# Laying out a stack of queries and its maxima by DMA through DRAM scratch instead of by selection products

## The chip, the cores and the metric

The kernel runs on one core of one Trainium2 chip. The metric is device time in microseconds of one launch. In the profile PE is TensorE (matrix products), PEld its weight loads, DVE VectorE, ACT ScalarE, POOL GpSimd, and SP is SyncE, which here issues every DMA.

## The reference

Sixteen sequences of 256 tokens with 128 channels go through four layers, each with a layer norm ahead and a residual behind: a linear attention with decay ("a"), a feed-forward layer ("ffn"), a causal softmax attention ("b"), and the same feed-forward layer again. The change lies in attention b:

```python
q = (x @ Wq + bq).reshape(Bx, Tx, HEADS, HD)      # 16 heads of 8
k = (x @ Wk + bk)[:, :, None, :]                  # one key head for all
v = (x @ Wv + bv)[:, :, None, :]
q, k = _apply_rope(q, sin, cos, HD), _apply_rope(k, sin, cos, HD)
att = jnp.einsum('bthd,bThd->bhtT', q, k) / math.sqrt(HD)
att = jax.nn.softmax(jnp.where(causal, -jnp.inf, att), axis=-1)
out = jnp.einsum('bhtT,bThd->bthd', att, v).reshape(Bx, Tx, Cx)
return out @ Wo + bo
# ffn: acc = sum over 8 experts of (silu(x @ wg) * (x @ wu)) @ wd, hidden size 512
```

## The kernel before

The 4096 tokens are cut into NT = 8 tiles of TOK = 512 tokens (two sequences, SPT = 2). The feed-forward layers set the pace: each tile passes through 8 experts x 4 chunks of 128 hidden columns = 32 units (UNIT), and the whole program is one list of slots, one unit per slot. Units 0 to 255 are the first feed-forward layer, then come 4 slots without a unit (GAP), then units 256 to 511. In each slot TensorE does the three gate products of its unit (point 0 follows), the three up products (point 1), and the three down products of the unit three slots back (point 2, LAG = 3). Every operand is split in a high part, rounded to float32r, and a low part, the rest, so each product is three.

The two attentions are fitted in between. A table gives every step of a tile a slot r, counted from the tile's own slot 0 (for b that is b_slot(t)), a point in the slot and a bank of PSUM (A_CELL L134, B_CELL L138). Slots -22 to 35 of one b tile overlap with those of the next, 32 slots later. Each engine walks the slots in order and, within a slot, runs its parts in the order in which its loop names them; waits on semaphores do the rest. Nothing is reordered by a planner.

A b tile, in slots r: layer norm and its turn (-22 to -19); q, k and their rope partners projected (-8 to -6); VectorE multiplies by the cosine and sine tables (`rope_b`), GpSimd adds the two (QK, -6 and -5, L624), ScalarE rounds to the high half (QKH, -5 and -4, L807), VectorE subtracts for the low half (QKL, -4 and -3, L1414). The heads have 8 channels, so a product over one head would use 8 of 128 rows. Instead the kernel stacks, for each of four groups g of 32 partitions (RG), the parts high, high, low of one head's query (8 rows each, 24 in all) and two rows for a maximum; the keys stand beside it as high, low, high and two rows of ones. One product over 32 rows then gives the exact sum and, in the second pass, subtracts the row's maximum. Four heads j lie side by side in the columns.

These stacks are made by selection products: `query_stack` (L1097, cells qst0 to qst3, slots -3 and -2) and `key_stack` (L1102, cell kst, slot -1) multiply by matrices of ones and zeros in SELR, and ScalarE copies the result to QST (L812) and KST (L816). `rows` (slots 0 to 11) then computes the masked scores by rows, VectorE takes their negated maxima (L1362) and splits them into a zeroed tile NMP (`split_maxima`). `stack2` (L1070, four cells per tile, slots 7, 9, 14, 15) adds to a copy of QST the turned maxima, by products with an identity, and ScalarE copies that to Q2 (L828). `cols` (slots 12 to 23) computes the scores again by columns, with the maximum subtracted; ScalarE takes the exponential (`exps`), GpSimd cuts what lies above the diagonal (`cut_weights` L595), and `values` (slots 18, 19, 24, 25) multiplies by v.

GpSimd's loop over the slots (L689 to L697) runs, in each slot, the low half HL of the unit one slot back (`hidden_lo` L536), then its part of attention a, then that of b with the cuts. SyncE reloads the weights of one expert (1.5 MB, L512) as soon as the down products have freed one of three buffers, in a plain loop over the loads, and stores a finished tile now and then. The loads fall in the slots r = -6, -2, 2, 6, ... of a b tile.

Of the kernel before, what the change touches and what calls it, by code (L numbers as in the profile page):

```python
# [14 lines left out]
P = 128  # L15
# [13 lines left out]
RG = 32  # L29
# [7 lines left out]
def constants():  # L37
# [24 lines left out]
    r = np.arange(P)  # L62
    c["mask_rows"] = np.where(r[None, :] > r[:, None], MASKED, 0.0)
    c["mask_cols"] = np.where(r[:, None] > r[None, :], MASKED, 0.0)

    for j in range(NJ):
        hi = np.zeros((P, P), np.float32)
        lo = np.zeros((P, P), np.float32)
        for g in range(NG):
            for x in range(DB):  # L70
                src = (NJ * g + j) * DB + x
                hi[src, RG * g + x] = hi[src, RG * g + DB + x] = lo[src, RG * g + 2 * DB + x] = 1
        c[f"qhi_{j}"], c[f"qlo_{j}"] = hi, lo
    hi = np.zeros((P, P), np.float32)
    lo = np.zeros((P, P), np.float32)
    for g in range(NG):
        for x in range(DB):
            hi[x, RG * g + x] = hi[x, RG * g + 2 * DB + x] = lo[x, RG * g + DB + x] = 1
    c["khi"], c["klo"] = hi, lo
    ones = np.zeros((P, P), np.float32)  # L80
    for g in range(NG):
        ones[0, RG * g + 3 * DB:RG * g + 3 * DB + 2] = 1
    c["kone"] = ones
    c["eye"] = eye
# [11 lines left out]
C_SEL = CPOS["qhi_0"][0]  # L96
SELS = [f"q{p}_{j}" for j in range(NJ) for p in ("hi", "lo")] + ["khi", "klo", "kone", "eye"]
# [30 lines left out]
def unit_of(g):  # L128
# [10 lines left out]
          "qst0": (-3, 1, 0), "qst1": (-3, 2, 1), "qst2": (-2, 1, 2), "qst3": (-2, 2, 0), "kst": (-1, 1, 1),  # L139
          ("stack", 0, 0): (7, 1, 3), ("stack", 0, 1): (9, 1, 3), ("stack", 1, 0): (14, 1, 3),  # L140
          ("stack", 1, 1): (15, 1, 3), ("pv", 0, 0): (18, 1, 3), ("pv", 0, 1): (19, 0, 3), ("sums", 0, 0): (20, 1, 3),
# [70 lines left out]
def program(nc, a_x, a_Wq, a_Wk, a_Wv, a_Wbeta, a_bbeta, a_Wmix, a_bmix, a_Wout, a_bout, a_ln_g, a_ln_b,  # L212
            b_Wq, b_bq, b_Wk, b_bk, b_Wv, b_bv, b_Wo, b_bo, f_Wg, f_Wu, f_Wd, consts, out):
    ctx = ExitStack()
    with ctx:
# [31 lines left out]
        ONESR = sb("ONESR", [1, TOK], F32R)  # L247
# [9 lines left out]
        SELR = sb("SELR", [P, 2 * NJ + 4, P], F32R)  # L257
# [27 lines left out]
        kept_sel = nc.dram_tensor("kept_sel", [P, len(SELS) * P], F32)  # L285
# [10 lines left out]
        def here(name, offset, *shape, dt=F32):  # L296
# [38 lines left out]
        NMP = take("NMP", 2, 2, NJ, P, dt=F32R)  # L335
# [6 lines left out]
        Q2 = take("Q2", 2, NJ, SEQ, dt=F32R)  # L342
# [12 lines left out]
        ld = sems("ld", "x0 x1 x tables masks sel0 sel wa wb ba bb raw0 raw1")  # L355
# [7 lines left out]
        B = sems("b", "proj roped u_q u_k hi lo v_ready v_used st_ready st_used kst_ready kst_used row_ready row_used nmh nml "  # L363
                      "q2_ready q2_used t_ready t_used t_cut pv os turn ro o ot otc out biased done")
# [62 lines left out]
        def consumed(key):  # L427
# [15 lines left out]
            if name in ("qst0", "qst1", "qst2", "qst3"):  # L443
                return B.st_used, NJ * t + int(name[3]) + 1
            if name == "kst":
                return B.kst_used, t + 1
            if name == "v":
# [4 lines left out]
                    "stack": lambda: (B.q2_used, 2 * n + name[2] + 1),  # L452
# [20 lines left out]
        def _(sp):  # L473
# [15 lines left out]
            sp.dma_start(kept_sel[:, :], consts[:, C_SEL:]).then_inc(ld.sel0, 16)  # L489
# [8 lines left out]
            sp.wait_ge(ld.sel0, 16)  # L498
            sp.dma_start(SELR[:, :, :].rearrange("p a b -> p (a b)").bitcast(F32), kept_sel[:, :]).then_inc(ld.sel, 16)
            sp.dma_start(MRAW[:, :, :].rearrange("p a b -> p (a b)"), consts[:, C_MASK:C_SEL]).then_inc(ld.masks, 16)  # L500
# [5 lines left out]
            for x in range(NE, 2 * NT * NE):  # L506
# [6 lines left out]
                if x % NE == 4 and x // NE > NT:  # L513
                    t = x // NE - NT - 1
                    sp.wait_ge(F.done, NT + t + 1)
                    sp.dma_start(o_tok[:, t], X[:, t, :, :]).then_inc(stored, 16)
# [5 lines left out]
        def _(g):  # L522
# [85 lines left out]
            def side_b(t, r):  # L608
# [16 lines left out]
                for b in range(SPT):  # L625
                    for i, (at, point) in enumerate(COLS_AT[b]):
                        if r == at + (point == 2) + 1:
                            cut_weights(SPT * t + b, i)
# [3 lines left out]
            def early(slot):  # L632
# [33 lines left out]
                if slot == first + 7:  # L666
                    g.tensor_copy(ONESR[:, 0:P], ONES[0:1, :]).then_inc(pr.mask, 1)
                    for k in range(1, SUB):
                        g.tensor_copy(ONESR[:, k * P:(k + 1) * P], ONES[0:1, :]).then_inc(pr.mask, 1)
# [9 lines left out]
                if slot == a_slot(NT - 1) + 10:  # L679
                    g.wait_ge(A.proj, len(PROJ) * NT)  # L680
                    g.memset(NMP[:, :, :, :, :].rearrange("p a b c d -> p (a b c d)").bitcast(F32),
                             0.0).then_inc(pr.zero, 1)
                    g.memset(VF[:, :, :], 0.0).then_inc(pr.zero, 1)
# [5 lines left out]
            for slot in range(G_FIRST, G_LAST + 1):  # L689
                n = unit_of(slot - 1)  # L690
                if n is not None and on_pool(n):
                    hidden_lo(n)
                for t, r in a_tiles(slot):
                    side_a(t, r)
                for t, r in b_tiles(slot):
                    side_b(t, r)
                early(slot)  # L697

        @block.scalar
        def _(act):  # L700
# [94 lines left out]
            def side_b(t, r):  # L795
# [7 lines left out]
                if r in (-5, -4):  # L803
                    i = r + 5
                    act.wait_ge((B.u_q, B.u_k)[i], t + 1)
                    after(act, B.kst_ready, t)
                    act.activation(QKH[:, i, :], QK[:, i, :], ACT.Copy).then_inc(B.hi, 1)  # L807
                for j, at in enumerate((-3, -2, -2, -1)):
                    if r == at:
                        act.wait_ge(B.st_ready, NJ * t + j + 1)  # L810
                        after(act, B.q2_ready, 4 * t)
                        act.activation(QST[:, j, :], sbank[bank_of(("b", t, f"qst{j}"))], ACT.Copy).then_inc(B.st_used, 1)  # L812
                if r == -1:
                    act.wait_ge(B.kst_ready, t + 1)
                    after(act, B.t_ready, 8 * t)
                    act.activation(KST[:, :], sbank[bank_of(("b", t, "kst"))], ACT.Copy).then_inc(B.kst_used, 1)  # L816
                for b in range(SPT):
# [6 lines left out]
                    for h in range(2):  # L824
                        if r == B_CELL["stack", b, h][0]:
                            act.wait_ge(B.q2_ready, 2 * n + h + 1)
                            after(act, B.t_ready, 4 * (n - 1))
                            act.activation(Q2[:, b, 2 * h:2 * h + 2, :], r3(sbank[bank_of(("b", t, ("stack", b, h)))], 2),  # L828
                                           ACT.Copy).then_inc(B.q2_used, 1)
# [18 lines left out]
            for slot in range(G_FIRST, G_LAST + 1):  # L848
# [22 lines left out]
                if slot == a_slot(NT - 1) + 11:  # L871
                    act.wait_ge(pr.zero, 2)
# [6 lines left out]
        def _(pe):  # L879
            SQ, SL, SK, SKL, SKONE, SID = 0, 1, 2 * NJ, 2 * NJ + 1, 2 * NJ + 2, 2 * NJ + 3  # L880
# [124 lines left out]
            def rows(t, b, i):  # L1005

                if (b, i) == (0, 0):
                    pe.wait_ge(B.kst_used, t + 1)
                    pe.wait_ge(B.st_used, NJ * (t + 1))
                q = [QST[g * RG:(g + 1) * RG, :, b * SEQ:(b + 1) * SEQ] for g in range(NG)]  # L1010
                ks = [KST[g * RG:(g + 1) * RG, b * SEQ:(b + 1) * SEQ] for g in range(NG)]
# [11 lines left out]
            def cols(t, b, i):  # L1023

                n = SPT * t + b
                if i == 0:
                    pe.wait_ge(B.q2_used, 2 * (n + 1))
                for x, (part, g) in enumerate(THREES[i]):
                    rg = slice(g * RG, (g + 1) * RG)
                    key = KST[rg, b * SEQ + P:(b + 1) * SEQ] if part == 0 else KST[rg, b * SEQ:b * SEQ + P]  # L1030
                    q2 = Q2[rg, b, :, P:SEQ] if part == 0 else Q2[rg, b, 2 * (part - 1):2 * part, :]
# [38 lines left out]
            def stack2(n, b, h, bk):  # L1070

                pe.wait_ge(B.nml, 2 * (n + 1))
                for x in range(2):
                    j = 2 * h + x
                    dst = bk[:, x * SEQ:(x + 1) * SEQ]
                    pe.matmul(dst, SELR[:, SID, :], QST[:, j, b * SEQ:(b + 1) * SEQ], start=True, stop=False)  # L1076
                    for a in range(2):
                        m = pe.matmul(dst[:, a * P:(a + 1) * P], NMP[:, b, a, j, :], SELR[:, SID, :],  # L1078
                                      start=False, stop=(a == 1))
                m.then_inc(B.q2_ready, 1)  # L1080
# [16 lines left out]
            def query_stack(t, j, bk):  # L1097
                pe.wait_ge(B.lo, 2 * t + 1)
                pe.matmul(bk, SELR[:, SQ + 2 * j, :], QKH[:, 0, :], start=True, stop=False)
                pe.matmul(bk, SELR[:, SL + 2 * j, :], QKL[:, 0, :], start=False, stop=True).then_inc(B.st_ready, 1)  # L1100

            def key_stack(t, bk):  # L1102
                pe.wait_ge(B.lo, 2 * (t + 1))
                pe.matmul(bk, SELR[:, SK, :], QKH[:, 1, :], start=True, stop=False)
                pe.matmul(bk, SELR[:, SKL, :], QKL[:, 1, :], start=False, stop=False)
# [441 lines left out]
```

## Time and profile before

| | |
|---|---|
| median of 3 runs | 1659.95 us (1657.62 to 1661.47) |
| the profiled execution, its own time | 1660.08 us |
| its span, first to last instruction | 1658.4 us |
| TensorE's mean granted clock | 0.976 of full |
| PE, DVE, ACT, POOL busy | 1506.3, 1174.4, 886.4, 792.4 us |
| GpSimd's HL, waiting for ScalarE's HH | 550.2 us in 266 waits |
| DMA engines, mean busy share | 36% |

Busy time of TensorE is modelled: a product of 512 columns is shown with some 0.39 us, but the starts of two in a row lie 0.23 us apart, since they are pipelined. So times of products are read from start to start. A wait in the tables is named by the instruction that waited and by the one that ended the wait.

### The profile page before, as it was taken

What the parts mean: (1) busy time and instruction counts of PE and PEld (TensorE: products, weight loads), DVE (VectorE), ACT (ScalarE), POOL (GpSimd) and SP (SyncE); (2) the same over time, 40 slices, a digit from 0 to 9 for tenths busy, and PEclk for the clock granted to TensorE, in tenths of its full rate; (3) what the DMA queues carried; (4) which work ended last, traced back from release to release, by engine and by line L of the source; (5) the groups of instructions that cost most, each with busy time, mean ns of one, the idle gap of its engine ahead of it and who ended that gap; (6) DMA issues with size and microseconds to landing.
All of it is one profiled execution on the core that took longest, in us unless ns stands there. A gap on an engine that the chain in (4) does not pass through costs nothing. (4 is left out here: it accounts for less than half of the span.)

```text
span 1658.4 us, 23396 instructions
## 1 busy us (share of the span) xinstructions
PE 1506.3 (91%) x7528; PEld 1115.0 (67%) x7528; DVE 1174.4 (71%) x1943; ACT 886.4 (53%) x1520; POOL 792.4 (48%) x742
## 2 busy tenths in 40 slices
PE   2478999899999998899999999999999999999998
PEld 2366777677777777676666776766767677676676
DVE  4778787868787787878685584765847658477565
ACT  2245556464655555455646555565555555655554
POOL 2636444643525253433226545455465554645565
PEclk9689999999999999999999999999999999999999
DMA  6305543433433343433323332333333323333353
GB/s 193 124 1 185 201 153 115 153 119 148 153 140 128 148 152 120 153 115 118 126 99 115 115 136 104 148 121 115 115 121 121 129 103 150 121 115 122 140 178 115
DMA packets 36238, 216.68 MB, mean 131 GB/s; under 512 B 3476, under 2 KB 17301, under 8 KB 19733
## 3 DMA queue, kind: packets, MB, share of 16 engines
q1 hardware_dynamic: 36116, 215.18, 35.6%
q8 instruction: 62, 1.02, 0.2%
q14 instruction: 60, 0.48, 0.1%
HBM read 200.49 MB, written 15.47 MB: 130 GB/s over the span
## 5 line engine op out<-in xcount | busy, mean ns | idle before, releaser
L539 POOL TENSOR_TENSOR HL<-HF,HH 128x512 fp32r<-128x512 f32 x312 | 415.6, 1332 | 554.8 <-ACT HH L719 550.2
L1233 DVE TENSOR_TENSOR HF<-SG,bank 128x512 f32<-128x512 f32 x512 | 350.0, 684 | 169.1 <-PE bank L886 87.6
L884 PE MATMUL bank<-XTH,W 128*128 128x512 f32 x1024 | 423.6, 414 | 10.4 <-ACT SG L712 9.9
L886 PE MATMUL bank<-XTH,W 128*128 128x512 f32 x1024 | 403.8, 394 | 0.0
L885 PE MATMUL bank<-XTL,W 128*128 128x512 f32 x1024 | 403.3, 394 | 0.0
L1216 DVE SCALAR_TENSOR_TENSOR SG<-SG,bank 128x512 f32<-128x512 f32 x288 | 197.1, 684 | 242.9 <-ACT SG L714 241.2
L714 ACT ACTIVATE SG<-bank 128x512 f32<-128x512 f32 x288 | 172.2, 598 | 322.1 <-PE bank L886 320.6
L719 ACT ACTIVATE HH<-HF 128x512 fp32r<-128x512 f32 x512 | 320.2, 625 | 35.1 <-DVE HF L1233 31.1
L712 ACT ACTIVATE SG<-bank 128x512 f32<-128x512 f32 x224 | 133.6, 596 | 247.6 <-PE bank L886 246.3
L884 PEld LDWEIGHTS bank<-XTH,W 128*128 128x128 f32 x1024 | 194.5, 190 | 82.6 <-issue 22.5
L884 PE MATMUL dbank<-HH,W 128*128 128x512 f32 x512 | 218.9, 427 | 14.6 <-DVE HL L1222 13.4
L886 PEld LDWEIGHTS bank<-XTH,W 128*128 128x128 f32 x1024 | 194.2, 190 | 43.6
L885 PEld LDWEIGHTS bank<-XTL,W 128*128 128x128 f32 x1024 | 194.9, 190 | 35.8
L886 PE MATMUL dbank<-HH,W 128*128 128x512 f32 x512 | 202.3, 395 | 0.0
L885 PE MATMUL dbank<-HL,W 128*128 128x512 f32 x512 | 202.0, 394 | 0.0
L1222 DVE TENSOR_TENSOR HL<-HF,HH 128x512 fp32r<-128x512 f32 x200 | 166.8, 834 | 0.0
L884 PEld LDWEIGHTS dbank<-HH,W 128*128 128x128 f32 x512 | 97.4, 190 | 54.8 <-DVE HL L1222 18.0
L1362 DVE TENSOR_REDUCE NM<-three 128x12 f32<-128x1536 f32 (+2 forms) x96 | 114.1, 1216 | 13.0 <-PE three L1019 7.5
L1269 DVE TENSOR_TENSOR_SCAN S<-BETA,KV 128x512 f32<-128x512 f32 x80 | 117.7, 1476 | 0.1
L886 PEld LDWEIGHTS dbank<-HH,W 128*128 128x128 f32 x512 | 97.1, 190 | 21.7
L576 POOL TENSOR_TENSOR S<-S,PQ 128x512 f32<-128x512 f32 x40 | 62.9, 1576 | 95.1 <-DVE S L1269 95.1
L885 PEld LDWEIGHTS dbank<-HL,W 128*128 128x128 f32 x512 | 97.7, 191 | 13.9
(219 smaller groups left out, 1813.3 us busy)
## 6 DMA issues: line engine op xcount, KB each, us to landing
W<-kept_w SPq DMA_DIRECT2D x120, 1536.0 KB, 6.3
kept_w<-W SPq DMA_DIRECT2D x8, 1536.0 KB, 6.2
X<-in_L_attn_a_x_dram SPq DMA_DIRECT2D x8, 256.0 KB, 5.9
WS<-in_L_ffn_Wg_dram SPq DMA_DIRECT2D x8, 256.0 KB, 6.5
WS<-in_L_ffn_Wu_dram SPq DMA_DIRECT2D x8, 256.0 KB, 6.8
WS<-in_L_ffn_Wd_dram SPq DMA_DIRECT2D x8, 256.0 KB, 7.1
out_dram<-X SPq DMA_DIRECT2D x8, 256.0 KB, 7.2
CST<-in_tables_dram SPq DMA_DIRECT2D x1, 896.5 KB, 4.9
```

The lines of the kernel that those rows point to most:

```text
L539: g.tensor_tensor(HL[:, n % HRING, :], HF[:, n % HFRING, :], HH[:, n % HRING, :].bitcast(F32), ALU.subtract).then_inc(F.hl, 1)
L712: act.activation(SG[:, n % 2, :], fbank[2 * n % 3], ACT.Silu).then_inc(F.sil, 1)
L714: act.activation(SG[:, n % 2, :], fbank[2 * n % 3], ACT.Tanh, scale=0.5).then_inc(F.sil, 1)
L719: act.activation(HH[:, n % HRING, :], HF[:, n % HFRING, :], ACT.Copy).then_inc(F.hh, 1)
L884: pe.matmul(dst, wh, xh, start=start, stop=False)
L885: pe.matmul(dst, wh, xl, start=False, stop=False)
L886: return pe.matmul(dst, wl, xh, start=False, stop=stop)
L1216: v.scalar_tensor_tensor(gated, gated, 1.0, fbank[2 * n % 3], ALU.add, ALU.mult).then_inc(F.half, 1)
L1222: v.tensor_tensor(HL[:, n % HRING, :], HF[:, n % HFRING, :], HH[:, n % HRING, :].bitcast(F32), ALU.subtract).then_inc(F.hlv, 1)
L1233: v.tensor_tensor(HF[:, n % HFRING, :], gated, fbank[(2 * n + 1) % 3], ALU.mult).then_inc(F.mul, 1)
L1269: v.tensor_tensor_scan(S[:, m, c, :], BETA[:, m, :], KV[:, c, :], 0.0, ALU.mult, ALU.add).then_inc(A.scan, 1)
L1362: v.tensor_reduce(dst, src, AX.X, ALU.max, negate=True).then_inc(B.row_used, 1)
```

## The change

The tables of selection matrices and their SBUF tile SELR, NMP, Q2 and the row of ones go. Two scratch tensors in DRAM come (kept_q, kept_m), and three columns in the tables. The queries' high and low halves are stored to kept_q by SyncE and fetched back, rearranged, into QST: eight transfers for the high half, four for the low. The keys, which the projection already repeats on all partitions, are made in place: VectorE forms QK or QK - QKH by a column of factors, and ScalarE scales and adds ones by two more columns. The maxima are split side by side (NMS), turned by one product per sequence, copied by ScalarE to MT, stored to kept_m and fetched into the two free rows of QST itself, in four transfers per sequence. `rows` and `cols` take 24 and 26 rows of a group. SyncE's loop goes by slots. In GpSimd's loop the cuts and its part of b stand ahead of HL.

```diff
 B_CELL = {... "v": (-5, 1, 1),
-          "qst0": (-3, 1, 0), "qst1": (-3, 2, 1), "qst2": (-2, 1, 2), "qst3": (-2, 2, 0), "kst": (-1, 1, 1),
-          ("stack", 0, 0): (7, 1, 3), ("stack", 0, 1): (9, 1, 3), ("stack", 1, 0): (14, 1, 3),
-          ("stack", 1, 1): (15, 1, 3), ("pv", 0, 0): ...
+          ("mx", 0): (7, 1, 3), ("mx", 1): (14, 1, 3), ("pv", 0, 0): ...
+        kept_q = nc.dram_tensor("kept_q", [2, P, TOK], F32)
+        kept_m = nc.dram_tensor("kept_m", [SPT, 32, SEQ], F32)
...
+            def spread_queries(t, part, src, done):
+                for g in range(NG):
+                    to = RG * g + DB * part
+                    rows = kept_q[src, RG * g:RG * (g + 1), :].rearrange("(j x) t -> x j t", j=NJ)
+                    sp.dma_start(QST[to:to + DB, :, :].bitcast(F32), rows).then_inc(done, 16)
+            def spread_maxima(n, b):
+                sp.wait_ge(B.mt_out, 32 * (n + 1))
+                rows = kept_m[b].rearrange("(r g j) t -> g r j t", r=2, g=NG)
+                for g in range(NG):
+                    to = RG * g + 3 * DB
+                    sp.dma_start(QST[to:to + 2, :, b * SEQ:(b + 1) * SEQ].bitcast(F32),
+                                 rows[g]).then_inc(B.mrow, 16)
+            def side_b(t, r):
+                if r == -5:
+                    sp.wait_ge(B.hi, 2 * t + 1)
+                    after(sp, B.st_hi, 8 * 16 * t)
+                    sp.dma_start(kept_q[0], QKH[:, 0, :].bitcast(F32)).then_inc(B.hi_out, 16)
+                if r == -4:
+                    sp.wait_ge(B.hi_out, 16 * (t + 1))
+                    after(sp, B.t_ready, 8 * t)
+                    spread_queries(t, 0, 0, B.st_hi)
+                    spread_queries(t, 1, 0, B.st_hi)
+                    sp.wait_ge(B.lo, 2 * t + 1)
+                    after(sp, B.st_lo, 4 * 16 * t)
+                    sp.dma_start(kept_q[1], QKL[:, 0, :].bitcast(F32)).then_inc(B.lo_out, 16)
+                if r == -3:
+                    sp.wait_ge(B.lo_out, 16 * (t + 1))
+                    spread_queries(t, 2, 1, B.st_lo)
+                for b in range(SPT):
+                    n = SPT * t + b
+                    if r == B_CELL["mx", b][0]:
+                        sp.wait_ge(B.mt, n + 1)
+                        after(sp, B.mrow, 4 * 16 * (n - 1))
+                        for a in range(2):
+                            sp.dma_start(kept_m[b, :, a * P:(a + 1) * P],
+                                         MT[32 * a:32 * (a + 1), b, :].bitcast(F32)).then_inc(B.mt_out, 16)
+                    if r == B_CELL["mx", b][0] + 1:
+                        spread_maxima(n, b)
+            for slot in range(0, G_LAST + 1):
+                for t, r in b_tiles(slot):
+                    side_b(t, r)
+                for x in range(NE, 2 * NT * NE):
+                    u = FC * (x - WRING + 1) - 1
+                    if slot == ffn_slot(u // UNIT) + u % UNIT + LAG:
+                        load_weights(x)
...
@@ gpsimd
             for slot in range(G_FIRST, G_LAST + 1):
+                for t, r in b_tiles(slot):
+                    ... cut_weights(SPT * t + b, i) where r == at + (point == 2) + 1
+                    side_b(t, r)
                 n = unit_of(slot - 1)
                 if n is not None and on_pool(n):
                     hidden_lo(n)
                 for t, r in a_tiles(slot):
                     side_a(t, r)
-                for t, r in b_tiles(slot):
-                    side_b(t, r)
@@ scalar
-                        act.activation(QST[:, j, :], sbank[bank_of(("b", t, f"qst{j}"))], ACT.Copy).then_inc(B.st_used, 1)
-                    act.activation(KST[:, :], sbank[bank_of(("b", t, "kst"))], ACT.Copy).then_inc(B.kst_used, 1)
+                if r == -2:
+                    act.wait_ge(B.lo, 2 * (t + 1))
+                    act.activation(KST[:, :], B1[:, 1, :], ACT.Identity, bias=cst("k_one"),
+                                   scale=cst("k_keep")).then_inc(B.kst_used, 1)
+                    if r == B_CELL["mx", b][0]:
+                        act.wait_ge(B.mx, n + 1)
+                        act.activation(MT[0:64, b, :], sbank[bank_of(("b", t, ("mx", b)))][0:64, 0:P],
+                                       ACT.Copy).then_inc(B.mt, 1)
@@ tensor, rows
                     pe.wait_ge(B.kst_used, t + 1)
-                    pe.wait_ge(B.st_used, NJ * (t + 1))
-                q = [QST[g * RG:(g + 1) * RG, :, b * SEQ:(b + 1) * SEQ] for g in range(NG)]
+                    pe.wait_ge(B.st_hi, 8 * 16 * (t + 1))
+                    pe.wait_ge(B.st_lo, 4 * 16 * (t + 1))
+                q = [QST[g * RG:g * RG + 3 * DB, :, b * SEQ:(b + 1) * SEQ] for g in range(NG)]
@@ tensor, cols
-                    pe.wait_ge(B.q2_used, 2 * (n + 1))
+                    pe.wait_ge(B.mrow, 4 * 16 * (n + 1))
-            def stack2(n, b, h, bk): ...
+            def turn_maxima(n, b, bk):
+                pe.wait_ge(B.nml, n + 1)
+                pe.transpose(bk[0:64, 0:P], NMS[:, b, :].bitcast(F32), ident).then_inc(B.mx, 1)
-            def query_stack(t, j, bk): ...
-            def key_stack(t, bk): ...
@@ vector, split_b
+                else:
+                    v.scalar_tensor_tensor(B1[:, 1, :], QKH[:, 1, :].bitcast(F32), cst("k_lo"),
+                                           QK[:, 1, :], ALU.mult, ALU.add).then_inc(B.lo, 1)
```

## Rows read from the trace of the kernel before

**Rows 1.** Page part 1: busy us (share of the span) and instructions

```profile
PE 1506.3 (91%) x7528; PEld 1115.0 (67%) x7528; DVE 1174.4 (71%) x1943; ACT 886.4 (53%) x1520; POOL 792.4 (48%) x742
```

**Rows 2.** One tile's stretch: PE, PEld, DVE, ACT, POOL busy; clock, DMA share, GB/s

```profile
966.00:1072.00 106.00, 102.19 (x566) 72.88 (x563) 69.12 (x121) 59.78 (x100) 56.78 (x54) 1.00 0.33 122
```

**Rows 3.** Waits of TensorE from 730 to 1560: us, times, longest

```profile
PE abank L1039 <- POOL PT L605: 21.7, 14, 1.7
PE three L1099 <- DVE QKL L1414: 2.6, 7, 0.7
...
PE three L1099 <- DVE XTL L1210: 1.7, 1, 1.7
```

**Rows 4.** Timeline of TensorE, slots -3 to 0: start, length, instruction [idle before]

```profile
936.88 0.47 PE L1099 MATMUL three<-QKH,SELR 128*128 128x512 f32 x1 [0.30 <-DVE QKL L1414]
...
938.56 0.40 PE L1099 MATMUL three<-QKH,SELR 128*128 128x512 f32 x1
...
939.03 0.39 PE L884 MATMUL bank<-XTH,W 128*128 128x512 f32 x1
...
943.41 0.39 PE L1104 MATMUL three<-QKH,SELR 128*128 128x512 f32 x1
...
944.39 0.50 PE L884 MATMUL dbank<-HH,W 128*128 128x512 f32 x1
...
947.24 0.82 PE L999 MATMUL three<-MASKB 128*128 128x512 bf16 x3
```

**Rows 5.** Timeline of TensorE, two groups of maxima products and what follows

```profile
967.46 0.28 PE L1076 MATMUL abank<-QST,SELR 128*128 128x256 f32 x1
...
968.09 0.45 PE L884 MATMUL dbank<-HH,W 128*128 128x512 f32 x1
...
974.01 0.38 PE L1076 MATMUL abank<-QST,SELR 128*128 128x256 f32 x1
...
974.74 0.44 PE L884 MATMUL dbank<-HH,W 128*128 128x512 f32 x1
```

**Rows 6.** Timeline of TensorE, four transposes and what follows

```profile
931.09 0.66 PE L1052 MATMUL abank<-CST,OS 128*128 128x128 f32 x4
931.50 0.48 PE L884 MATMUL dbank<-HH,W 128*128 128x512 f32 x1
```

**Rows 7.** Timeline of GpSimd ahead of a `values` cell

```profile
1000.22 1.28 POOL L539 TENSOR_TENSOR HL<-HF,HH 128x512 fp32r<-128x512 f32 x1 [1.05 <-ACT HH L719]
1001.46 0.86 POOL L605 TENSOR_SCALAR_AFFINE_SELECT PT<-PT 128x768 f32<-128x768 f32 x1
```

**Rows 8.** Timeline of ScalarE, the queries' high half

```profile
930.36 0.62 ACT L807 ACTIVATE QKH<-QK 128x512 fp32r<-128x512 f32 x1
```

**Rows 9.** Stretches during and behind a weight load, columns as in rows 2

```profile
930.50:933.50 3.00, 3.00 (x22) 2.75 (x22) 1.41 (x4) 0.48 (x1) 2.52 (x2) 1.00 0.96 397
934.50:942.50 8.00, 7.70 (x35) 6.02 (x35) 6.27 (x14) 4.83 (x10) 3.88 (x3) 1.00 0.00 0
```

**Rows 10.** Timeline of SyncE: two issues in a row, and the last store

```profile
6.48 0.43 SPq L482 DMA_DIRECT2D GB<-in_L_attn_a_ln_g_dram  x1
6.95 0.43 SPq L483 DMA_DIRECT2D GB<-in_L_attn_a_ln_b_dram  x1
...
1655.65 0.39 SPq L518 DMA_DIRECT2D out_dram<-X  x1
```

**Rows 11.** DMA issues: KB each, median us from issue to landing

```profile
WRAW<-in_L_attn_a_Wq_dram SPq DMA_DIRECT2D x1, 64.0 KB, 1.8
```

**Rows 12.** Stretches behind two idle times of TensorE, columns as in rows 2

```profile
732.00:734.00 2.00, 1.76 (x8) 1.45 (x9) 0.78 (x2) 0.60 (x1) 0.00 (x0) 1.00 0.00 0
...
184.00:189.30 5.30, 5.30 (x15) 4.20 (x14) 3.38 (x6) 2.76 (x6) 0.00 (x0) 0.50 0.25 104
```

**Rows 13.** Timeline of TensorE in that stretch: first and thirteenth of the products

```profile
184.09 0.78 PE L884 MATMUL dbank<-HH,W 128*128 128x512 f32 x1
...
189.36 0.41 PE L884 MATMUL bank<-XTH,W 128*128 128x512 f32 x1
```

More of the change, by code:

```diff
@@ L62, in constants @@
     r = np.arange(P)
+    part = r % RG // DB
+    c["k_lo"] = np.where(part == 1, -1.0, 0.0)[:, None]
+    c["k_keep"] = np.where(part < 3, 1.0, 0.0)[:, None]
+    c["k_one"] = np.where((r % RG == 3 * DB) | (r % RG == 3 * DB + 1), 1.0, 0.0)[:, None]
     c["mask_rows"] = np.where(r[None, :] > r[:, None], MASKED, 0.0)
     c["mask_cols"] = np.where(r[:, None] > r[None, :], MASKED, 0.0)
[L66 to L84, printed above, removed]
     return {k: np.asarray(v, np.float32) for k, v in c.items()}
@@ L334, in program @@
         at["now"] = arena
-        NMP = take("NMP", 2, 2, NJ, P, dt=F32R)
+        NMS = take("NMS", 2, 64, dt=F32R)
+        MT = take("MT", 2, P, dt=F32R)
         VF = take("VF", SUB, RG)
@@ L442, in consumed @@
                 return bproj_read(t, name)
[L443 to L446, printed above, removed]
             if name == "v":
@@ L451, in consumed @@
                     "cols": lambda: (B.t_used, 4 * n + name[2] + 1),
-                    "stack": lambda: (B.q2_used, 2 * n + name[2] + 1),
+                    "mx": lambda: (B.mt, n + 1),
                     "pv": lambda: (B.os, 2 * n + name[2] + 1),
@@ L505, in _, with load_weights @@
             sp.dma_start(BRAW[:, C:], row(b_bk)).then_inc(ld.wb, 16)
-            for x in range(NE, 2 * NT * NE):
+            def load_weights(x):
                 sp.wait_ge(F.down, FC * (x - WRING + 1))
@@ new lines, in _ @@
+            for slot in range(0, G_LAST + 1):
[5 more added lines that the diff above has]
+                        load_weights(x)
+                        if x % NE == 4 and x // NE > NT:
+                            t = x // NE - NT - 1
+                            sp.wait_ge(F.done, NT + t + 1)
+                            sp.dma_start(o_tok[:, t], X[:, t, :, :]).then_inc(stored, 16)
@@ L665, in early @@
                     g.tensor_copy(MASKB[:, 1, :], ident).then_inc(pr.mask, 1)
[L666 to L669, printed above, removed]
                 if slot == first + 8:
@@ L689, in _ @@
             for slot in range(G_FIRST, G_LAST + 1):
+                for t, r in b_tiles(slot):
+                    for b in range(SPT):
+                        for i, (at, point) in enumerate(COLS_AT[b]):
+                            if r == at + (point == 2) + 1:
+                                cut_weights(SPT * t + b, i)
+                    side_b(t, r)
                 n = unit_of(slot - 1)
@@ L823, in side_b @@
                             act.activation(OS[:, z, :], abank, ACT.Copy).then_inc(B.os, 1)
[L824 to L829, printed above, removed]
+                    if r == B_CELL["mx", b][0]:
+                        act.wait_ge(B.mx, n + 1)
+                        after(act, B.mt_out, 32 * (n - 1))
+                        act.activation(MT[0:64, b, :], sbank[bank_of(("b", t, ("mx", b)))][0:64, 0:P],
+                                       ACT.Copy).then_inc(B.mt, 1)
                     if r == B_CELL["ot", b][0]:
@@ L1345, in maxima @@
             def maxima(n, b, i):
-                after(v, B.nml, 2 * (n - 1))
+                after(v, B.nml, n - 1)
                 v.wait_ge(B.row_ready, 4 * n + i + 1)
@@ L1374, in split_maxima @@
                 v.wait_ge(B.row_used, 6 * (n + 1))
[L1375 to L1383 removed]
+                after(v, B.mx, n - 1)
+                dst = NMS[:, b, :].rearrange("p (a r h) -> p a r h", a=2, r=2)
+                v.tensor_copy(dst[:, :, 0, :], NM[:, b, :, :]).then_inc(B.nmh, 1)
+                v.wait_ge(B.nmh, n + 1)
+                v.tensor_tensor(dst[:, :, 1, :], NM[:, b, :, :], dst[:, :, 0, :].bitcast(F32),
+                                ALU.subtract).then_inc(B.nml, 1)
             def gather_sums(n, a, bank):
```

97 lines of the change are left out of this document (20 added, 77 removed).

## The prediction, made before the changed kernel was run

> **What bounds the kernel now.** I read the page's engine table first: TensorE is busy for 91% of the span [rows 1]. An average over stages says little, so I next cut the span into stretches of one attention tile each. In one such stretch, 32 slots of some 3.3 us, TensorE is busy for 102.2 of 106 us at the full clock, VectorE for 69, ScalarE for 60, GpSimd for 57 [rows 2]. There are eight such tiles, and all that the change touches lies in them. So a product that goes there is worth its whole time, and a new wait of TensorE costs its whole time. The waits of TensorE in this part (from 730 us on) are few: 21.7 us in 14 waits for GpSimd's cut of the weights, 2.6 us in 7 for VectorE's low half of the queries [rows 3]. The program takes 1660.1 us by its own time, 1.7 more than the span; the median of three runs is 1659.95, so the sum needs no correction. About 0.2% (3.3 us) is what a measurement of this kernel tells from no change.
>
> **The change, part by part.**
>
> *Query stack.* Eight products of 512 columns per tile go. Two of them, with the next instruction's start, take 938.56 to 939.03 = 0.47 us [rows 4]; four pairs are 1.88 us. With them goes the wait for VectorE in front of the first (2.6 us in all).
>
> *Key stack.* Three products go, 943.41 to 944.39 = 0.98 us [rows 4], and the product behind them starts about 0.1 us late after the one-row operand: 1.08 us. In their place ScalarE scales by a column, where it copied; VectorE's second subtraction has one operand more. Both engines are at two thirds of the stretch or less.
>
> *Maxima.* Four groups of products per tile go; two of them took 0.63 and 0.73 us [rows 5], so 4 x 0.68 = 2.72. Two transposes come: four in the trace take 931.09 to 931.50 = 0.41 us [rows 6], so 0.1 us each, 0.2 per tile.
>
> Sum on TensorE: (1.88 + 1.08 + 2.72) x 8 = 45.4, less 1.7 for the transposes, plus 2.6: 46.3 us. Eight evacuations of ScalarE per tile and two small VectorE operations per sequence go too; neither engine is the bound, so I count them at nothing. What is late next where the stacks stood is VectorE, the next busiest [rows 2]: a few tenths per tile, by my estimate, which I leave in the range.
>
> *GpSimd's order.* The cut for a slot now stands ahead of that slot's low half HL. In the trace the HL from 1000.22 runs, and behind it from 1001.46 the cut for which TensorE waits [rows 7]. Before that HL, GpSimd waited 1.05 us for ScalarE, so the cut can begin 2.3 us sooner, more than the longest of the waits (1.7 [rows 3]). I take all 21.7 us. What is moved back by it is HL, by one cut (0.86 us [rows 7]) or, at r = -1, by the four small operations of a layer norm. HL is used two slots later, so this costs nothing; if that cover failed it would show as TensorE waiting for HL.
>
> All gains: 46.3 + 21.7 = 68.0 us, 8.5 per tile, which by themselves would give 1592.
>
> *The new path.* The queries now go out to DRAM and come back in twelve transfers, each into 8 partitions (four rows of 2 KB in each, 64 KB). Every step is on SyncE's queue and must land before the rows products of slot 0. In the tile that I followed they began at 947.24 [rows 4]; with 1.88 + 1.08 + 0.30 gone they could begin at 944.0. The chain behind that time:
> - ScalarE writes the high half from 930.36 to 930.98 [rows 8], and SyncE issues its store. The weight load of slot -6 is on the same queue ahead of it, and it moves data until 934.5, at 397 GB/s at its height [rows 9]. Then 256 KB at that rate and the signal: about 936.
> - SyncE waits for that and issues eight transfers; one issue takes 0.47 us on its queue, start to start [rows 10]. A 64 KB load lands 1.8 us after its issue [rows 11]; less its data, 1.6 us of latency. With s the time of one transfer, if they follow each other, the last lands at 937.6 + 8s.
> - The store of the low half (its data are there by 936.9 [rows 4]) is behind them, 0.8 us; SyncE waits for it, 0.1, then four transfers: 1.6 + 4s.
> So the stack is there at 940.1 + 12s, and TensorE stalls for 12s - 3.9 us in each tile.
>
> No row shows a transfer into 8 partitions, so s is bounded. From below by the issue, 0.47 us; then the store's own latency counts (the last store of the program was issued at 1655.65, 2.75 us before the end [rows 10]), the last of the twelve lands at about 945.8, and the stall is 1.8 us. From above by a partition's share of the weight load: 397 GB/s over 128 partitions is 24.8 GB/s for 8, so 64 KB take 2.64 us and the stall is 27.8. The lower row is as near in size as the upper is in place, so I take the middle by ratio, 1.11 us: a stall of 9.4 us.
>
> The Trainium skill ("SBUF — State Buffer", section "Door 1: The DMA port swizzle (why `[64,N]` ≈ `[32,N]`)") says that a transfer's rate follows the number of SBUF ports that its partitions reach, and gives 27.6 GB/s as measured for partitions 0 to 3, one port. Eight neighbouring partitions reach two by its map; my estimate from that figure is 55 GB/s, s = 1.19, a stall of 10.4 us and a total of 1695. No run here shows it yet; it speaks against the change.
>
> A stall of that length costs more than itself. After the two idle stretches around 180 to 183 us the granted clock was 0.50 from 184 to 189.3 [rows 12], that is 1.2 in place of 2.4 GHz, and twelve products from 184.09 to 189.36 [rows 13] took 5.3 us where they take 2.8: 2.5 us lost. So a tile loses 9.4 + 2.5 = 11.9 us, eight lose 95.2.
>
> *The maxima's transfers* are smaller (8 rows of 1 KB, into 2 partitions). For the first sequence they have from slot 8 to slot 12. For the second they are issued in slot 15 behind a weight load (6 us) and are wanted late in slot 18, over 9 us later. I count no stall; if the cover failed, the first cols product would show it. The weight load of slot -2 now is issued behind the second set of transfers, up to 8 us later; it is wanted at slot 4, which the stall moves back as well. Nothing.
>
> The sum: 1660.1 - 68.0 + 95.2 = 1687.3, say 1687 us.
>
> **The rivals.**
>
> *The transfers run as fast as they are issued* (the faster side). The place is the first rows product of each tile, the price 12s - 3.9 us, and it decides below s = 0.83, where the stall with its clock (8.5 us) equals the gain. For it: 64 KB land in 1.8 us in this kernel, the DMA engines rest for most of a tile (0 GB/s from 934.5 to 942.5 [rows 9]). Against: that load goes to 128 partitions. The stall is 1.8 us per tile, too short for the clock to fall with any certainty (1.7 us of waiting [rows 3] before 732.24 left it at full [rows 12]). Time: 1592 + 14 = 1606; with the clock lost each time 1626.
>
> *A partition takes no more than it got in the weight load.* For it: that is the only rate into a partition that a row shows. Against: there all 128 were filled at once. s = 2.64, 27.8 + 2.5 = 30.3 us per tile: 1592 + 242 = 1834.
>
> *Gain and stall cancel* (s around 0.83): within a few us of 1660. Nothing speaks for it but that it lies between.
>
> **How the numbers follow.** The forecast, with s from 0.9 to 1.4, has 0.52; its own range is 1660 to 1725 (s = 0.9: 6.9 + 2.5 us per tile, 1667; s = 1.4: 12.9 + 2.5, 1715; both with some us either way for the gains). Transfers at the rate of issue have 0.33, the partition's share 0.10, the cancelling 0.05. Faster is the second case and a little of the last: 0.35; the same 0.03; slower 0.62. The range of 1600 to 1730 leaves out the partition's share and the faster half of the second case's spread, under 2 in 10.
>
> **What would show it.** Right: at the first rows product (its mask product) of each tile TensorE waits some 10 us for a DMA that writes QST, eight times, and the granted clock is half behind it; the twelve transfers follow each other at about 1.1 us; the waits for GpSimd's cut are gone; no TensorE wait for HL or for the maxima's rows. Wrong: no wait there, or one of under 4 us, and a time near 1606, or one of 25 us and more. It would also be wrong, whatever the time, if TensorE's wait stood at the cols products, or if its busy time fell by clearly less than 40 us.

## The result, and the profile after

The changed kernel takes 1688.23 us (median of 4 runs, 1686.86 to 1693.65); the kernel before took 1658.78 (4 runs) on the same chip: ratio 1.0185, interval 1.0154 to 1.0216. It is slower by 29 us, where 1687 was forecast. The profiled execution took 1687.45 us, its span is 1685.5, TensorE's mean granted clock 0.946 (before 0.976).

The engine table of the page after answers to [rows 1]:

```profile
PE 1484.4 (88%) x7264; PEld 1090.9 (65%) x7264; DVE 1171.4 (70%) x1911; ACT 855.6 (51%) x1472; POOL 790.9 (47%) x737
```

264 products are gone: the work that was to go did go. TensorE's busy time still fell by 21.9 us only, since some of the products that are left ran slower. The stretch of one tile, at [rows 2]'s times, shows the clock at 0.95 and 97 us of products in 106:

```profile
966.00:1072.00 106.00, 97.03 (x518) 68.94 (x515) 68.84 (x116) 55.92 (x94) 56.75 (x53) 0.95 0.41 127
```

TensorE's waits from 730 to 1560 us (total, times, longest) answer to [rows 3]. The line below is all new; a line for GpSimd's cut (PT) or for VectorE's QKL there is none.

```profile
PE three L1011 <- DMA QST<-kept_q: 69.7, 8, 9.4
```

In the tile that begins near 935 us, the timelines of SyncE and then of TensorE (start, length, instruction) show how that wait is made:

```profile
941.50 0.32 SPq L507 DMA_DIRECT2D kept_q<-QKH  x1
946.53 2.70 SPq L493 DMA_DIRECT2D QST<-kept_q  x8
949.33 0.34 SPq L515 DMA_DIRECT2D kept_q<-QKL  x1
956.91 1.30 SPq L493 DMA_DIRECT2D QST<-kept_q  x4
958.25 26.24 SPq L487 DMA_DIRECT2D W<-kept_w  x3
```

```profile
954.18 0.40 PE L898 MATMUL dbank<-HH,W 128*128 128x512 f32 x1
963.59 1.44 PE L1011 MATMUL three<-MASKB 128*128 128x512 bf16 x3 [9.01 <-DMA QST<-kept_q]
964.96 1.12 PE L1029 MATMUL three<-KST,QST 24*128 24x128 f32 x12
966.01 0.80 PE L896 MATMUL bank<-XTH,W 128*128 128x512 f32 x1
...
969.44 0.78 PE L896 MATMUL dbank<-HH,W 128*128 128x512 f32 x1
970.01 0.44 PE L897 MATMUL dbank<-HL,W 128*128 128x512 f32 x1
```

The store of the high half is waited for 5.0 us; then eight transfers, the low store behind them, landing after 7.6 us, and four transfers more. TensorE stands from about 954.6 to 963.59, and up to 970 its products start 0.43 us apart in place of 0.23. The granted clock fell during the wait and stayed half behind it (columns as in [rows 2]; the DMA share adds up the times of all packets and divides by the time of 16 engines, so where packets overlap it passes 1):

```profile
958.00:959.00 1.00, 0.00 (x0) 0.00 (x0) 0.00 (x0) 0.00 (x0) 0.00 (x0) 1.00 0.56 98
959.00:960.00 1.00, 0.00 (x0) 0.00 (x0) 0.00 (x0) 0.00 (x0) 0.00 (x0) 0.93 1.12 139
960.00:961.00 1.00, 0.00 (x0) 0.00 (x0) 0.00 (x0) 0.00 (x0) 0.00 (x0) 0.50 1.37 147
```

### The profile page after: what moved, and what is told of

Its sections match the earlier page's. It is cut to its first block and busy times, and to the rows that moved or that the text cites. A ratio compares the mean times of both kernels' runs of the same rounds, so it can differ in the third digit from the quotient of the medians.

```text
span 1685.5 us, 22927 instructions
## 1 busy us (share of the span) xinstructions
PE 1484.4 (88%) x7264; PEld 1090.9 (65%) x7264; DVE 1171.4 (70%) x1911; ACT 855.6 (51%) x1472; POOL 790.9 (47%) x737
## 5 line engine op out<-in xcount | busy, mean ns | idle before, releaser
L896 PEld LDWEIGHTS bank<-XTH,W 128*128 128x128 f32 x1024 | 196.7, 192 | 86.3 <-issue 26.2
L898 PEld LDWEIGHTS bank<-XTH,W 128*128 128x128 f32 x1024 | 196.3, 192 | 44.4
```

The lines of the kernel that those rows point to most:

```text
L896: pe.matmul(dst, wh, xh, start=start, stop=False)
L898: return pe.matmul(dst, wl, xh, start=False, stop=stop)
```

## The experiments

Each time stands beside runs of the kernel before on the same chip (medians 1656.89 to 1659.96). Waits are the totals of TensorE for the queries' transfers, in eight tiles.

### Is it the bytes into 8 partitions?

**Same bytes, 32 partitions.**

```diff
-  rows = kept_q[src, RG*g:RG*(g+1), :].rearrange("(j x) t -> x j t", j=NJ)
-  sp.dma_start(QST[to:to + DB, :, :].bitcast(F32), rows)
+  sp.dma_start(DUM[RG*g:RG*(g+1), part, :], kept_q[src, RG*g:RG*(g+1), :])
```

> Edit: each of the twelve transfers of the queries keeps its source, its 64 KB and its place in the queue, but writes 32 partitions (one row of 2 KB each) of a spare tile, not 8 partitions (four rows each) of QST. QST holds zeros in its query rows, so the scores are left out of the result. Theory W (the width of the destination sets the time s of one transfer): the transfers go as fast as they are issued, 0.34 us; high store landed 5.0 us after its issue as now, eight issues, low store landed 2.7 us after its own, four issues and 1.8 us: the stack is there at most 2 us after TensorE could begin. Wait 0 to 2 us per tile in place of 8.7, full clock, 1688 - 8 x (8.7 + 2.9) + 8 x 1 = 1603 us (1594 to 1612). Rival L (the detour itself costs: two stores, two waits on SyncE, twelve issues): wait 8 to 9 us per tile, 1688 us. Rival Q (the weight load ahead on the queue costs): the same 1688 us.

Measured: 1613.66 us, ratio 0.9739 (0.9711 to 0.9767). The wait is 15.0 us, 1.9 per tile:

```profile
PE three L1013 <- DMA DUM<-kept_q: 15.0, 8, 3.1
```

The transfers go as fast as they are issued, 0.46 us from start to start. That is the first rival of the prediction, within a tenth of a us (1.8 per tile), when the 8 partitions are taken away. The place and the queue are the same, so the place by itself is not what costs. In three tiles, behind waits of 2.7 to 3.1 us, the clock still fell for a while (0.62 to 0.81 in the 9 us behind), and the time is just above the expected range. The edit changes two things at once: a transfer writes 32 partitions, and it has 32 outermost rows where it had 8.

**Half the bytes.**

```diff
-  sp.dma_start(QST[to:to + DB, :, :].bitcast(F32), rows)
+  sp.dma_start(QST[to:to + DB, 0:2, :].bitcast(F32), rows[:, 0:2, :])
```

> Edit: each of the twelve transfers carries two of the four heads of its group, 32 KB in place of 64, into the same 8 partitions; the other two heads' query rows stay zero and are left out. Theory W: s falls from about 1.05 to 0.55 us, the stall of 12 s - 3.9 by 6 us to some 2.7 (1.5 to 4); 1688 - 8 x 6 = 1640 us if the clock still falls behind it, 1617 if it doesn't. Rival L: a transfer costs the same whatever it carries, wait 8 to 9 us, 1688 us. Rival Q: the same 1688 us.

Measured: 1603.78 us, ratio 0.9679 (0.9647 to 0.9712); wait 9.2 us, below what was expected. With 32 KB the issue is the pace (0.34 us from start to start), not half of s.

**Four wide transfers**, 24 partitions each, from a layout in DRAM that has the stack's rows; then the same with the low half a slot sooner.

```diff
+  rows = kept_q[DB*part:DB*(part+1), :, :].rearrange("x h t -> h x t")   # store, three times
+  sp.dma_start(rows, src[:, 0, :].bitcast(F32))
+  sp.dma_start(QST[RG*g:RG*g + 3*DB, :, :].bitcast(F32), kept_q[:, NJ*g:NJ*(g+1), :])
```

> The changed kernel with the queries laid out in DRAM scratch as the stack wants them (24 rows by 16 heads: high half stored twice, low half once), so that four transfers of 192 KB into 24 partitions each fill the whole stack where twelve of 64 KB into 8 partitions did; all four start behind the low half's store, one slot after it. Same bytes into the stack. Theory W (the time goes by the bytes for each written partition, that is by how many partitions a transfer writes at once): the three rows of one group go side by side, one third of the time, about 1.0 to 1.3 us each, 4 to 5 us for four; the stack is there at about the time TensorE comes to it: wait 0 to 3 us per tile, 1594 to 1622 us. Rival I (the time goes by the bytes, or by the bytes of DRAM rows, whatever the partitions): four transfers take what twelve took, 12 us, and start later: wait over 9 us per tile, over 1690 us.

> As the kernel with four wide transfers, and VectorE's low half and its store also one slot earlier (the slot in which the high half is made), so that the four transfers start some 3 us sooner. Theory W: no wait for the stack is left, the clock stays at full behind it, and all of the forecast gains stand: 1590 to 1600 us. Rival (the earlier low half delays other work of VectorE, or TensorE then waits for VectorE or GpSimd instead): as the kernel with four wide transfers or 3 to 15 us above it.

Measured: 1637.76 us, ratio 0.9875 (0.9858 to 0.9892), wait 28.8 (3.6 per tile); with the low half sooner 1620.40, ratio 0.9751 (0.9705 to 0.9797), wait 14.1. Both miss the expected times by some 16 to 20 us. Theory W has the direction right and the size too good.

**Without the load behind them.** The weight load of slot -2 is cut, first in the wide kernel, then in the changed one.

```diff
-  sp.dma_start(w_slot(x), kept_w[x % NE])
+  if short: sp.dma_start(w_slot(x)[:, 0:16], kept_w[x % NE][:, 0:16])   # r in (-3, -2)
+  else:     sp.dma_start(w_slot(x), kept_w[x % NE])
```

> The kernel with four wide transfers into 24 partitions each, with the weight load that is issued right behind them (eight slots of the run, one per tile) cut to 16 of 3072 columns; the feed-forward's result is wrong in those slots. Theory B (the load behind, which writes all 128 partitions, takes part of the DMA engines' time from the stack's transfers): wait per tile from 3.6 to 1 to 2 us and 1605 to 1622 us. Rival (the four are slow by themselves, about 2 us each whatever runs behind): wait as it was, 3.6 us, 1634 to 1640 us.

> The changed kernel with the weight load that is issued right behind the low half's four transfers cut to 16 of 3072 columns (eight slots of the run; the feed-forward's result is wrong in those). Theory B: the four take 6.4 us beside the load and would take 256 KB at the 60 GB/s of the high half's, 4.3 us, without it: wait per tile from 8.7 to about 6.6 us, half clock behind it as before, 1668 to 1676 us. Rival (the load behind takes nothing): 1685 to 1691 us.

Measured: the wide one 1630.21 us, ratio 0.9821 (0.9801 to 0.9840), wait 15.6 in place of 28.8; the changed one 1682.38, ratio 1.0134 (1.0118 to 1.0151), wait 61.5 in place of 69.7. So the load behind takes 1.0 to 1.7 us of a tile's transfers: half of what was expected in the changed kernel, whose time lies between the two expected ranges, and what was expected in the wide one, whose time did not follow (see the last section). Alone, the last four small transfers took from the first issue at 955.36 to TensorE's start at 961.08, 5.72 us. In the trace their packets run from 956.23 to 959.64: 3.41 us, s = 0.85 us, 77 GB/s. The other 2.3 us are latency, where the prediction used 1.6. The wide ones took 6.89 us, their packets 5.09: 1.27 us each for three times the bytes, 154 GB/s.

**The load ahead of the high store cut**, in the same way at r = -6.

> Edit: the one weight load per tile that stands ahead of the high half's store on the queue (slot -6) fetches 16 of its 3072 columns; that expert's weights are then partly those of another, which the result shows. Theory W: the high store lands 2.5 us after its issue in place of 5.1, all behind it is 2.6 us sooner; wait 6.1 us per tile, the clock still falls, 1688 - 8 x 2.6 = 1667 us. Rival Q (the place in the queue is most of the stall): wait under 3 us, about 1615 us. Rival L: the wait shrinks by 2.6 as well, so this run tells Q from the other two only.

Measured: 1661.47 us, ratio 1.0031 (1.0015 to 1.0046), wait 43.3. The high store lands 2.0 us after its issue in place of 5.1. That is 3.3 us per tile of the 8.7; the queue ahead is a part, not the cause.

**One transfer into all 128 partitions**, the four groups in one, 1 MB.

```diff
-  for g in range(NG):
-      sp.dma_start(QST[RG*g:RG*g + 3*DB, :, :]..., kept_q[:, NJ*g:NJ*(g+1), :])
+  rows = kept_q.rearrange("r (g j) t -> g r (j t)", g=NG)        # kept_q has 32 rows now
+  sp.dma_start(QST[:, :, :].rearrange("p j t -> p (j t)").bitcast(F32), rows)
```

> The kernel with wide transfers and the earlier low half, but with all four groups laid out in DRAM scratch with their eight unused rows, so that one transfer of 1 MB into all 128 partitions takes the place of four of 192 KB into 24 each (a third more bytes; the unused rows hold input data that no product reads, and the maxima's two rows among them are written later, as before). Theory W (the time goes by how many partitions are written at once): a weight load of 1.5 MB into 128 partitions lands in 6.5 us, so 1 MB takes some 4.4; issued at the place of the four, it is there before TensorE comes: no wait, clock at full behind it, 1590 to 1602 us. Rival I (time by bytes): the four took about 7.7 us for 786 KB, so 1 MB takes 10 us, TensorE waits 4 us per tile, about 1640 us.

Measured: 1736.23 us, ratio 1.0460 (1.0439 to 1.0482), wait 117.8: both theories are refuted. **Eight partitions that lie apart**:

```diff
-  to = RG * g + DB * part
-  sp.dma_start(QST[to:to + DB, :, :].bitcast(F32), rows)
+  to = NG * part + g
+  sp.dma_start(DUM[to:P:P // DB, :, :], rows)
```

> The changed kernel with the queries' twelve transfers of 64 KB, each still into 8 partitions with the same row shape (8 rows of 4 pieces of 2 KB), but into 8 partitions that lie 16 apart in a spare tile, where the change writes 8 neighbours; the stack itself holds zeros. It tells two causes of the slow transfers apart. Theory P (8 neighbouring partitions take only so many bytes a second together; far apart ones take more): the transfers go about as fast as those into 32 partitions did, wait 0 to 2.5 us per tile, clock mostly at full, 1603 to 1622 us. Theory D (a transfer is dealt out to as many DMA engines as it has outermost rows, eight of 16 here, whose share is 0.5 to 0.6 in the windows, as it is 0.22 to 0.31 where the one transfer of 1 MB has four; each engine has its own pace): pace as in the change, 60 GB/s, wait 7 to 9 us per tile, 1680 to 1690 us. Both in part: between them, with the share telling how many engines work (0.5 or less).

Measured: 1656.59 us, ratio 0.9982 (0.9972 to 0.9993), wait 40.2: between the two. The stretches in which such transfers ran tell the causes apart (columns as in [rows 2]; the last two are DMA share and GB/s). 8 neighbours, in the changed kernel (the low half's store is queued behind the eight fetches, and its bytes count too), then in its run without the load behind: a part of the last four transfers, and all four:

```profile
951.00:955.00 4.00, 3.58 (x15) 2.36 (x13) 3.70 (x13) 2.96 (x6) 2.86 (x6) 1.00 0.55 61
```

```profile
957.00:959.00 2.00, 0.00 (x0) 0.00 (x0) 0.00 (x0) 0.00 (x0) 0.00 (x0) 0.50 0.59 73
956.20:959.70 3.50, 0.00 (x0) 0.00 (x0) 0.00 (x0) 0.00 (x0) 0.00 (x0) 0.50 0.51 77
```

8 partitions 16 apart:

```profile
941.70:944.70 3.00, 3.00 (x15) 2.47 (x14) 2.91 (x8) 2.47 (x5) 1.55 (x2) 1.00 0.32 106
```

24 neighbours (load behind cut), then 32 neighbours:

```profile
936.30:940.30 4.00, 3.21 (x14) 2.05 (x12) 3.46 (x11) 2.96 (x7) 2.85 (x6) 1.00 0.79 179
```

```profile
927.00:930.00 3.00, 3.00 (x15) 2.46 (x14) 2.91 (x6) 1.95 (x4) 1.77 (x2) 1.00 0.53 145
```

All 128 partitions by one transfer with four outermost rows:

```profile
975.00:983.00 8.00, 0.00 (x0) 0.00 (x0) 0.00 (x0) 0.00 (x0) 0.00 (x0) 0.50 0.25 76
```

Two limits show. The same eight rows, put into partitions that lie apart, move 106 GB/s with a share of 0.32, where neighbours move 61 with 0.55, 73 with 0.59 or 77 with 0.51. A DMA engine's busy time carries 2.2 to 3 times the bytes (106 / 0.32 against 77 / 0.51, 73 / 0.59 and 61 / 0.55), so neighbours hold each other up. And the single transfer with four outermost rows shows a share of 0.25, as four engines of 16 would, though it writes 128 partitions. That the share follows the outermost rows is read from these three values (4, 8 and 24 rows: 0.25, 0.51 to 0.59, 0.79) and was not varied by itself. With partitions apart the issue takes 0.61 us each (eight in 4.90 us, against 2.70); why is open. 64 KB in 0.61 us is 107 GB/s, so the 106 is the pace of the issue and only a lower bound of the transfers' own. It waits 3.1 us per tile more than the run into 32 partitions; twelve issues of 0.61 in place of 0.46 us are 1.8 of that. Whether its eight outermost rows cost anything there is not shown.

The Trainium skill ("DMA: Bandwidth & Descriptors", section "Why a DMA increments its semaphore by 16 and not by 1") says that a transfer is split over the largest number of engines up to 16 that divides the slowest dimension of both its sides: 4, 8 and 12 of 16 here, 0.25, 0.50 and 0.75, which the shares bear out within 0.1. The Trainium skill's page "SBUF — State Buffer" ("Door 1: The DMA port swizzle (why `[64,N]` ≈ `[32,N]`)") gives 8 and 24 neighbours two and six ports and partitions 16 apart four, by my estimate from its 27.6 GB/s for one port 55, 166 and 110 GB/s. For 8 and 24 neighbours 61 to 77 and 154 to 179 were measured, which agrees in order and roughly in size; the 106 for partitions apart, set by the issue, tests nothing.

### Is the rest of the loss the clock?

```diff
+  for k in range(32):        # ahead of the wait for the stack; overwritten by the masks
+      pe.matmul(three[:, k % 3, :], WBH[:, 0, :], XH[:, :], start=True, stop=True, ...)
```

> Edit: ahead of its wait for the stack TensorE does 32 products of 512 columns per tile whose results are overwritten (7.4 us at full clock, inside the wait of 8.7). Theory K (the half clock behind the stall comes from the idle time, and costs 2.9 us per tile): the granted clock stays at 1.00 from the stall on, 1688 - 8 x 2.9 = 1665 us, with 256 products more. Rival (the slow slots behind the stall come of something else, such as refilling the pipeline between the engines): 1688 us or some us more, the products behind the stall as slow as now.

Measured: 1670.00 us, ratio 1.0086 (1.0049 to 1.0122): 256 products more than the changed kernel and 18 us faster. The stack comes no sooner, but the same products behind it run at full clock, 3.49 us from 960.00 to 963.49 where the changed kernel took 6.42 (963.59 to 970.01). In two of the eight tiles, where 2.9 and 3.4 us of waiting were left behind the added products, the clock still fell for a while (0.81 in the 9 us behind). The tile of the timelines above:

```profile
950.95 7.49 PE L1022 MATMUL three<-XH,WBH 128*128 128x512 f32 x32
960.00 0.81 PE L1011 MATMUL three<-MASKB 128*128 128x512 bf16 x3 [1.56 <-DMA QST<-kept_q]
...
963.18 0.47 PE L896 MATMUL dbank<-HH,W 128*128 128x512 f32 x1
963.49 0.39 PE L897 MATMUL dbank<-HL,W 128*128 128x512 f32 x1
```

### The other parts of the change

**GpSimd's old order**: in its loop HL and attention a stand ahead of the cuts again.

> The changed kernel with one part undone: GpSimd works again in the old order within a slot (hidden low halves, stage A, then stage B's side work, then the cuts of the weights). Theory (the cut's wait cost its whole time): TensorE waits again for the cut, about 20 us in some 14 waits, and the time is that of the changed kernel plus about 20, 1704 to 1710 us. Rival (with a long wait for the stack in every tile there is slack, so the cut is done in time in part): fewer than 10 us of such waits, 1688 to 1697 us. If GpSimd's order had done nothing for the time: 1688.

Measured: 1708.86 us, ratio 1.0300 (1.0285 to 1.0316), 20.6 above the changed kernel (19.6 if each is set against the kernel before on its own chip), as expected, with the waits back:

```profile
PE abank L1053 <- POOL PT L629: 22.4, 14, 1.8
```

**The queries' stack by selection products again**, the rest as changed:

```diff
-  ... spread_queries(t, 0, 0, B.st_hi); spread_queries(t, 1, 0, B.st_hi); ... (t, 2, 1, B.st_lo)
+  pe.matmul(bk, SELR[:, 2 * j, :], QKH[:, 0, :], start=True, stop=False)
+  pe.matmul(bk, SELR[:, 2 * j + 1, :], QKL[:, 0, :], start=False, stop=True)
+  act.activation(QST[:, j, :], sbank[...], ACT.Copy)
```

> The changed kernel with one part undone: the queries' stack comes from selection products and ScalarE's four evictions again, as before the change; the key stack without products, the maxima by DMA and GpSimd's new order stay. Theory (all that is lost is lost in the queries' path through DRAM, and the other three parts gain what was forecast): no wait for a transfer of the queries; the granted clock in the stretch behind the former wait stays at full; TensorE's time falls from the kernel before by 8.7 us (key stack) and about 20 us (maxima) of products and by about 20 us of waits for the cut: 1608 to 1615 us. Rival (the clock and some wait elsewhere take part of it back): 1630 to 1660 us.

Measured: 1608.21 us, ratio 0.9692 (0.9677 to 0.9706), clock 0.977, no wait for a transfer of the queries. It is the fastest complete version, ahead of both kernels.

## Why the prediction was right

**The gains.** 68.0 us were forecast. Spans differ by 1685.5 - 1658.4 = 27.1 us; the waits cost 69.7 and the clock 8 x 2.93 = 23.4, if each tile loses to it what the tile above lost; so the gains are about 69.7 + 23.4 - 27.1 = 66.0. Followed in every tile to the second HL product behind the wait, against the half-bytes run, the clock takes 1.7 to 3.3 us, 24 in all; 1.7 of that the kernel before lost too, at a clock of 0.50 from 851.6 to 855.0, so the sum stands within 1 us. Two measurements stand by themselves: GpSimd's order 20.6 (forecast 21.7), and key stack, maxima and order together 1659.76 - 1608.21 = 51.6 (8.7 + 20.0 + 21.7 = 50.4). The query stack's own gain (1.88 x 8 + 2.6 = 17.6 forecast) was not isolated; what is left for it is 66.0 - 51.6 = 14.4. No wait for HL by GpSimd was added and none at the cols products. The wait for HL by VectorE grew, before and after:

```profile
PE dbank L884 <- DVE HL L1222: 1.6, 2, 1.2
PE dbank L896 <- DVE HL L1213: 5.0, 3, 2.2
```

With GpSimd's old order it is 4.0, so that order is at most a small part of it; the cause is open.

**The chain to the stack.** From ScalarE's high half written (941.48 in the tile above) the stack was forecast 22.4 us later and came 22.1 later (963.59). TensorE was ready after 13.1 (forecast 13.0). The pieces: store landed after 5.0 (forecast 5.0); from there to the low store landed 10.4 (forecast 11.4: 1.6 + 8s and the store with SyncE's step, 0.9); the last four 6.7 (forecast 6.0; with the load behind cut 5.7). So two pieces were off, by 1.0 and 0.7 us in opposite directions. The issue cost 0.34 us, not 0.47; it was not the pace.

**The choice of s.** This was the step with nothing under it but two far bounds. The mean wait, 8.71 us, gives by 12s - 3.9 an s of 1.05 us, where the middle by ratio was 1.11. That figure is no transfer's own time: the packets of the last four show 0.85 us with the load behind cut, and the latency there was 2.3 us, not 1.6, so a long s and a short latency made up for each other. The sum gave no mechanism for the middle; that neighbours hold each other up is what the strided run shows. That the middle came so near is luck, of the bounds and of these two errors. The chain named the load ahead of the high store and priced the store rightly with it (with the load cut the store lands in 2.0 us, and the wait is 3.3 us shorter); what it did not name is that the load issued behind takes 1.0 us.

**The clock.** 2.5 us per tile were forecast from one place in another part of the program; 2.93 were measured in the tile above and 3.0 on the mean of eight. It is the smaller term that was under-sized, and it made up for the shorter wait: 8 x (8.71 + 2.93) = 93.1 against 95.2.

**A sign that was put wrongly.** The prediction called itself wrong if TensorE's busy time fell by clearly less than 40 us. It fell by 21.9, yet the products went as forecast: busy time counts products at the clock they ran at, and the half clock lengthened those behind the wait. With half the bytes, and the same 7264 products, where the clock was full in seven of the eight tiles behind the wait, it is 1459.1, 47.2 below before. The sign should have been the number of products.

**The rivals.** Transfers at the rate of issue were a real case: 32 partitions gave the 1.9 us per tile and, at 1613.66, a time inside the 1606 to 1626 stated. Its condition, not its arithmetic, failed. The partition's share fell by the same rows: it gave 8 partitions 24.8 GB/s, and in the stretches shown they took 61 and more.

## What to carry to other kernels

Ask of a transfer how many neighbouring partitions it writes and how many outermost rows it has before counting its bytes: 64 KB took 0.85 us into 8 neighbours, with nothing large behind, and 0.46 us, the issue's time, into 32; that four outermost rows cost bandwidth rests on one run. A step that leaves the bound engine for a chain of a store, a wait, a fetch and a wait on one queue needs the whole chain ahead of its use; here it was 22 us with 13 to spare. And take the parts of a change apart: three of its four were worth 51.6 us together, hidden behind the fourth.

## What the runs showed that was not expected

A short wait of TensorE decides the clock unevenly. In one execution of the wide kernel with the early low half the waits of eight tiles were 0.6 to 2.3 us; a wait of 1.88 us left the clock at full in the 9 us behind it, one of 1.93 did not (columns: busy, clock, DMA share, GB/s):

```profile
941.65:950.65 9.00, 9.00 (x56) 1.00 0.33 120
1040.45:1049.45 9.00, 9.00 (x43) 0.62 0.22 91
```

Its four runs spread from 1606.22 us (mean clock 0.976) to 1625.16 (0.964), far more than other kernels here. Nor does the length alone decide across kernels: with 32 partitions a wait of 2.20 us left the clock at full, with half the bytes one of 1.81 did not. In the wide kernel with the load cut, waits of 2.2 to 2.7 us halved the clock in six of eight tiles (in a seventh it had halved 1.4 us ahead of a wait of 1.2), and where the load was left, waits of 3.0 to 4.7 us were followed by mean clocks of 0.50 to 0.81. To the second HL product behind the waits the clock took some 21 us with the load cut and 15 with it. That is why 13.2 us less of waiting gained it only 7.6. TensorE's busy time says the same: 1484.8 us with the load cut, 1476.7 with it, for as many products. What tells such waits apart is open.
